# A graph attention and normalisation kernel on one core: late sums and table parts moved, Q's last stores spread over the loads of Q, and four changes of order in the last stage

## What is computed

```python
Q, K, V = ((x @ W).reshape(N, 8, 64) for W in (Wq, Wk, Wv))
score = jnp.einsum('ehd,ehd->eh', K[src], Q[dst]) / 8
score = jnp.exp(jnp.clip(score, -5.0, 5.0))[..., None]
wV = jax.ops.segment_sum(V[src] * score, dst, num_segments=N)
Z = jax.ops.segment_sum(score, dst, num_segments=N)
h = x + (wV / (Z + 1e-06)).reshape(N, D)
mean = jnp.mean(h, axis=0)
var = jnp.mean(jnp.square(h - mean), axis=0)
y = (h - mean) * jax.lax.rsqrt(var + 1e-05) * bn_gamma + bn_beta
out = _layernorm(x + y, axis=-1)
```

## Time and profile before

| what | us |
|---|---|
| median of 3 runs | 1886.88 |
| lowest, highest | 1885.74, 1889.61 |
| the profiled execution | 1886.89 |
| its span, first to last instruction | 1885.0 |
| PE busy | 1843.9 (98%) |
| DVE busy | 1726.0 (92%) |
| ACT busy | 1427.3 (76%) |
| POOL busy | 1235.8 (66%) |
| DMA, mean of the span | 313 GB/s |

### The profile page before, as it was taken

How to read it: one execution, slowest core, us unless ns; L and a number is a source line. 1 busy time by engine, 2 the same in 40 slices (tenths; PEclk the granted TensorE clock), 3 DMA queues, 4 the chain that set the end, 5 groups by cost and what they waited for, 6 DMA issues and landing times.

```text
span 1885.0 us, 41041 instructions
## 1 busy us (share of the span) xinstructions
PE 1843.9 (98%) x7561; PEld 1290.4 (68%) x7672; DVE 1726.0 (92%) x2608; ACT 1427.3 (76%) x4699; POOL 1235.8 (66%) x1424
## 2 busy tenths in 40 slices
PE   8999999998999999999999999999999999999897
PEld 4444444446788887888888888888888888877333
DVE  8877776667999999999999999999999999999898
ACT  1112221126999999999999999999999999998867
POOL 1221112116888888888888888888888888875677
PEclk9999999998999999999999999999999999999999
DMA  5676667658999999999999999999999999999317
GB/s 207 221 252 223 223 222 247 235 195 316 365 364 358 354 356 357 372 357 360 349 365 373 348 354 358 368 357 357 345 368 362 361 360 353 369 360 370 118 34 290
DMA packets 191291, 589.09 MB, mean 313 GB/s; under 512 B 29104, under 2 KB 30864, under 8 KB 191248
## 3 DMA queue, kind: packets, MB, share of 16 engines
q0 software_dynamic: 135904, 465.14, 67.1%
q1 hardware_dynamic: 51888, 121.69, 17.8%
q10 hardware_dynamic: 3456, 1.78, 0.4%
HBM read 535.27 MB, written 78.91 MB: 326 GB/s over the span
## 4 chain that ended last, share of the span: by engine, by line
PE 57%; DVE 23%; issue 7%; DMA 7%; ACT 3%; POOL 2%; ACTq 1%; POOLq 0%; SPq 0%; DVEq 0%
PE places L390 21%; PE acc L1110 21%; PE q_ps L1094 12%; DVE kv L968 9%; DVE raw L979 7%; DMA kv<-kv_d,idx 5%; POOL kv L924 2%; DVE stats L1463 1%; ACT kv L1019 1%; DVE agg L1447 1%; PE mm_ps L1120 1%; DVE agg L1456 1%; DVE raw L972 1%; DMA q_tile<-xb_d 1%; DVE kv L886 1%
## 5 line engine op out<-in xcount | busy, mean ns | idle before, releaser
L924 POOL DMA_INDIRECT kv<-kv_d,idx x880 | 892.8, 1014 | 242.0 <-issue 202.9
L1019 ACT ACTIVATE kv<-kv 128x64 f32<-128x64 f32 x3520 | 889.1, 335 | 14.3
L1110 PE MATMUL acc<-kv,mm_rest 128*128 128x260 f32 x2640 | 634.6, 383 | 3.5 <-POOL kv L886 2.2
L1110 PEld LDWEIGHTS acc<-kv,mm_rest 128*128 128x128 f32 x2640 | 489.9, 189 | 105.1 <-issue 27.7
L968 DVE TENSOR_TENSOR kv<-q_ps,kv 128x1024 f32<-128x1024 f32 x440 | 536.5, 1219 | 16.5 <-DMA kv<-kv_d,idx 10.7
L979 DVE TENSOR_REDUCE raw<-kv 128x16 f32<-128x1024 f32 x440 | 533.1, 1212 | 0.0
L1094 PE MATMUL q_ps<-q_tile,mm_rest 128*128 x1320 | 422.1, 441 | 5.1 <-DVE kv L968 4.9
L390 PE MATMUL places<-w_sb,s_sb 128*128 128x512 f32 x704 | 305.9, 593 | 3.4 <-issue 3.1
L1094 PEld LDWEIGHTS q_ps<-q_tile,mm_rest 128*128 128x128 f32 x1320 | 247.6, 189 | 53.7 <-DVE kv L968 10.4
L886 DVE TENSOR_TENSOR kv<-kv 128x384 f32<-128x384 f32 (+1 forms) x440 | 272.3, 619 | 0.0
L390 PEld LDWEIGHTS places<-w_sb,s_sb 128*128 128x128 f32 x704 | 133.1, 190 | 172.9 <-issue 165.3
(11 more groups left out here) (202 smaller groups left out, 1482.8 us busy)
## 6 DMA issues: line engine op xcount, KB each, us to landing
kv_d<-kv SPq DMA_DIRECT2D x98, 256.0 KB, 2.2
q_tile<-q_d SPq DMA_DIRECT2D x49, 512.0 KB
kv<-kv_d,idx POOLq DMA_INDIRECT x880, 6.4
xb<-in_x POOLq DMA_DIRECT2D x49, 256.0 KB, 4.2
xb_d<-xb POOLq DMA_DIRECT2D x49, 256.0 KB, 6.5
out_rows<-agg SPq DMA_DIRECT2D x49, 256.0 KB, 2.1
x_sb<-in_xT SPq DMA_DIRECT2D x16, 768.0 KB, 6.5
q_d<-q_c SPq DMA_DIRECT2D x16, 512.0 KB, 2.6
```

The costliest lines, as they stand in the source:

```text
L924: pool.indirect_dma_start(kv[:, s, u, 0:2 * DIM], None, kv_d, bass.IndirectOffsetOnAxis(idx[:, s, u:u + 1], 0), bounds_check=N_NODES - 1, ...
L1019: return act.activation(v, v, ACT.Copy, scale=kv[:, s, u, 2 * DIM + h:2 * DIM + h + 1])
L1110: last = pe.matmul(acc[:, bass.ds(par, 1), DIM - (1 - n) * HALF:DIM + n * HALF], m, kv[:, sc, u, DIM + n * HALF:DIM + (n + 1) * HALF], sta ...
```

## The change

Seven edits, which touch no amount of work but four sums.

In `project`: `x_sums_last(0)`, the sum T8 and `ends` are moved behind L753 of trio 0 (`ends` into part 0), and every part of the tables comes two places later, so that trio 0 has only part 0, at its end. SP no longer stores Q of the last trio and of LONE there.

In `attend`: SP loads Q's tiles 2 and 3, then stores the last trio's third tile once tile 3 has landed, and in the same way the three others after tiles 5, 7 and 9. Before the loads from tile 40 on it waits for these stores.

In `normalise`: four pairs more are added on POOL (places 36 with 38, 37 with 39, 40 with 42, 41 with 43) and taken by PE three places later; the last four sums of squares are in another order; the last group's root stands behind the first norm of the group before it; and rows 46 and 48 are normed on DVE, with a semaphore of their own.

```diff
+DVE_NORMS = (TILES - 3, TILES - 1)
@@ project, sync
-                if g == TRIOS - 1:
-                    sp.wait_ge(soft["s_g0"], 32)
-                store_q(c, split_of(g, 2), q_c, s_qc)
...
+                if g < TRIOS - 1:
+                    store_q(c, split_of(g, 2), q_c, s_qc)
...
-            store_q(LONE, TILES, q_d_lone, s_qc)
@@ project, vector
+            def weight_sums_last():
                 dve.tensor_tensor(weight(T8), weight(B11), weight(T13), ALU.add).then_inc(s_wt, 1)
-            def weight_sums_last():
...
-            x_sums_last(0)
-            dve.wait_ge(s_dl, 16)
-            tab(dve.tensor_tensor(ends[:, :], dl[:, :], k128[:, :], ALU.add))
...
-                tables(3 * g)
+                tables(3 * g - 2)
...
                 dve.wait_ge(s_dec, decoded(g, 5))
+                if g == 0:
+                    x_sums_last(0)
...
-                tables(3 * g + 1)
+                tables(3 * g - 1)
...
-                tables(3 * g + 2)
+                tables(3 * g)
@@ attend, sync
+            for n, (t, q, done) in enumerate(last_q):
+                with sp.Fori(2 + 2 * n, 4 + 2 * n) as u:
+                    load_in_turn(u)
+                sp.wait_ge(s_q, 16 * (4 + 2 * n))
+                sp.dma_start(q_d[t * P:(t + 1) * P, :], q[:, :, :].rearrange("p a n -> p (a n)")).then_inc(done, 16)
@@ normalise
+        LATE_PRES = [38, 39, 42, 43]
+            return p + (3 if p in LATE_PRES else AFTER)
...
+            pe.wait_ge(s_sq, TILES - 3)
+            squares(TILES - 4)
+            pe.wait_ge(s_sqp, n + 1)
+            squares(TILES - 6)
+            pe.wait_ge(s_sq, TILES)
+            squares(TILES - 1)
+            pe.wait_ge(s_sqp, n + 2)
+            squares(TILES - 3)
...
+                    if group_of(t) == g and t not in DVE_NORMS:
                         norm(t)
+                        if g == GROUPS - 2 and t == ENDS[g - 1]:
+                            root(g + 1)
...
+                if t >= TILES + 4:
+                    norm(DVE_NORMS[t - TILES - 4])
```

More of the change, by code:

```diff
@@ L54 @@
 SQ_RING = 7
+Q_KEPT = 40
 X_SLOTS = 6
@@ L598, in x_sums_first @@
                 dve.wait_ge(s_x[g % 2], trio_x(g))
+                if g == 1:
+                    dve.wait_ge(s_sums, summed(0, X7))
                 if g:
@@ L648, in tables @@
             def tables(n):
-                if n < VTILES:
+                if n == 0:
+                    dve.wait_ge(s_dl, 16)
+                    tab(dve.tensor_tensor(ends[:, :], dl[:, :], k128[:, :], ALU.add))
+                if 0 <= n < VTILES:
                     visits(n)
@@ L902, in _ @@
                 load(t)
+            sp.wait_ge(soft["s_tb"], 48)
+            for name in ("s_qa", "s_qb", "s_qc"):
+                sp.wait_ge(soft[name], 16 * (TILES // 3 - 1))
+            sp.wait_ge(soft["s_split"], TILES)
+            for n, (t, q, done) in enumerate(last_q):
[3 more added lines that the diff above has]
+                sp.dma_start(q_d[t * P:(t + 1) * P, :], q[:, :, :].rearrange("p a n -> p (a n)")).then_inc(done, 16)
+            with sp.Fori(2 + 2 * len(last_q), Q_KEPT) as t:
+                load_in_turn(t)
+            sp.wait_ge(soft["s_qa"], 16 * (TILES // 3))
+            sp.wait_ge(soft["s_qb"], 16 * (TILES // 3))
+            sp.wait_ge(soft["s_qc"], 16 * (TILES // 3 + 1))
+            with sp.Fori(Q_KEPT, TILES) as t:
+                load_in_turn(t)
             for t in range(FIRST_X):
@@ L1220, in sums_before_pre @@
         def sums_before_pre(k):
-            return sum(not in_pre(n) for n in range(pres[k] + AFTER + 1)) + k + 1
+            return sum(not in_pre(n) for n in range(due(pres[k]) + 1)) + k + 1
         def squares_used(t):
@@ L1263, in _ @@
             for t in range(TILES):
-                sp.wait_ge(s_o, t + 1)
+                if t in DVE_NORMS:
+                    sp.wait_ge(s_od, DVE_NORMS.index(t) + 1)
+                else:
+                    sp.wait_ge(s_o, t + 1 - sum(n < t for n in DVE_NORMS))
                 sp.dma_start(out[t * P:(t + 1) * P, :], row(t)).then_inc(s_out, 16)
@@ L1318, in _ @@
                               stop=p == TILES - 1).then_inc(s_sum, 1)
[L1319 to L1323, removed]
+                for k in range(len(pres)):
+                    if due(pres[k]) == p:
+                        pe.wait_ge(s_pre, k + 1)
+                        pe.matmul(mean_ps, ones[:, :], sq(k % SQ_RING), start=False,
+                                  stop=False).then_inc(s_sum, 1)
             def squares(t):
                 pe.matmul(var_ps, weights(t)[:, :], sq(t % SQ_RING), start=t == 0,
-                          stop=t == TILES - 1).then_inc(s_var, 1)
+                          stop=t == TILES - 3).then_inc(s_var, 1)
             n = 0
-            for t in range(TILES):
-                if t % FIVE == 0 or t == TILES - 1:
+            for t in range(TILES - 6):
+                if t % FIVE == 0:
                     pe.wait_ge(s_sq, t + 1)
@@ L1477, in offset, with norm @@
                                   negate=True).then_inc(s_sh, 1)
+            def norm(t):
+                dve.wait_ge(s_sh, group_of(t) + 1)
+                dve.tensor_scalar(row(t), line(t), mv[:, t, 1:2], shift[:, t:t + 1], ALU.mult, ALU.add).then_inc(s_od, 1)
             for t in range(TILES + 6):
@@ L1526, in program @@
         block = ctx.enter_context(nc.Block())
-        project(nc, block, xT, x, wq, wk, wv, beta, edges, dlast, xb_d, kv_d, q_d, t_d, cnt_d, lb_d, nb_d, tabs, kv, first, soft)
+        last_q = project(nc, block, xT, x, wq, wk, wv, beta, edges, dlast, xb_d, kv_d, q_d, t_d, cnt_d, lb_d, nb_d, tabs, kv, first, soft)
         agg = sb("agg", [P, TILES, AGG], F32)
```

30 lines of the change are left out of this document (14 added, 16 removed).

## The result

| what | us |
| --- | --- |
| before, median of 7 runs | 1886.88 |
| changed, median of 7 runs | 1892.22 (1890.80 to 1895.41) |
| ratio, with its 95% interval | 1.0032 (1.0022 to 1.0041) |
| profiled execution of the changed kernel: time, span | 1895.41, 1893.6 |

The change makes the kernel slower by 0.28% (5.3 us), a little more than the 0.2% that can be told. The time lies in the range on record, 2.8 us above the forecast of 1889.4, and on the slower side of 1890.7, not within 0.2% as the likeliest case had it.

The account below looks back on a forecast made before the run. The prediction took PE and DVE to set the pace together, PE alone in the first stage. Terms -3.05+8.5+1.7-4.8+1.0+0.7-0.3-1.2 = +2.55 on 1886.88 gave 1889.4 us, range 1883.5 to 1894.5.

Parts of the forecast that it names:

- signs of the stall: PE unpaused before 120 us, trio 4 additions waiting 10 us or more, PE idle 7 to 10 near 130, clock 0.5.
- Hole in trio 0: First stage, trio 0: PE's pause at 27.65 closes wholly once work moves behind L753, -3.05 us.
- rival 5: Trio 0: the hole had a slow start that goes with it, 1.65 us more, 1887.7 us; chance 0.02.
- Stall: Trio 4: PE waits for rows that POOL loads late, behind its later wait for `s_visit`, +8.5 us.
- The straight copy: Trio 4: POOL's chain copied at its traced lengths to the later release, PE standing still for 9.6 us.
- rival 3: Row loads land in trio 3's Q stores and next x load, stall 13.5 us, 1894.4 us; chance 0.14.
- Clock behind it: Trio 4: PE's clock falls after the long pause, +1.7 us (0 to 3.3).
- Q's stores: Second stage: moving them ends DVE's first gather waits, -4.8 us; their new place between loads costs +1.0.
- Rival 4: Second stage gives little: PE starts at the lower clock, stores between loads cost 2.8 us, 1892.9 us; chance 0.10.
- Four late pairs: Last stage, mean: no gain from four more POOL sums, a 2.8 us PE pause may drop the clock, +0.7 us.
- Squares: Last stage: the new order of the last squares lets PE go on while POOL sums, -0.3 us.
- End: Last stage: early last root and two rows on DVE relieve ACT by 1.8 us, less store and latency, -1.2 us.

Follow-up runs that it names:

- e1_rows_first: Changed kernel, but POOL does trio 3's row stores and loads before waiting for `s_visit` and making the tables; 2084.55 us, ratio 0.9985 to the kernel before.
- e7_first_stage_only: Kernel before with only the first-stage edits, and trio 3's rows ahead of the tables on POOL; 2082.53 us, ratio 0.9981.
- e5_change_again: Changed kernel run again, unedited, on another chip; 2093.47 us, ratio 1.0034 to the kernel before.
- e3_q_only: Kernel before with only Q's last four stores moved between the loads of Q's tiles; 2088.56 us, ratio 1.0001.
- group 3: Last runs, on one chip: small store on SyncE, trio 3's rows first without late pairs (Q's stores as before, or moved), kernel before; ratios 1.0008, 0.9980, 0.9979, 1.0003.
- the best kernel: Changed kernel with trio 3's rows first on POOL and without the four more pairs of the mean; 2081.37 us, ratio 0.9976 to the kernel before.
- e9_store_on_sp: Changed kernel, wait for the small `t_d` store and two loads moved behind trio 3's rows, that store issued by SyncE; 2068.43 us, ratio 1.0008.
- e12_before: Kernel before itself, unedited, run for its trace on another chip; 2067.10 us, ratio 1.0003.

## Why the prediction came out where it did

**What was right.** The change turns on one hidden link, the part that releases `s_visit`, and this link costs more than the closed hole brings. Forecast for the first stage: +7.15; measured +10.26. The signs of the stall are there: no pause of PE before 120 us, an addition that waits over 10 us for a row (15.55), an idle PE near 130, a clock of 0.50 behind it. Two are off in size: PE is idle for 11.21 us, not 7 to 10, and the fifth pair's multiply comes 2.5 us nearer, not 4.8. `e1_rows_first` shows that this is the cause: one moved call on POOL takes 13.5 us out of the stage.

**Step by step:**

- *Hole in trio 0, -3.05*: measured -3.5 (`e7_first_stage_only`), and -4.2 us in the median there. Right by that pair of traces; the half microsecond more is time in PE's rows about the hole. But rival 5, a slow start behind the hole, got a chance of 0.02 from one trace, and from a row of 28 to 30 us that ends before PE goes on at 30.70. It is in three of the five traces with the hole, at 1.5 to 1.7 us, near the 1.65 named.
- *Stall, +8.5*: measured 11.21 (9.69 in `e5_change_again`). This is the mis-sized term. The straight copy gave 9.6, and I took 1.1 off because the small store would stand behind less. It was not faster (wait 11.91, before 11.17), the rows' stores were waited for 5.15 instead of 3.06, and the last row landed in 4.36, near the 4.6 assumed. The discount had only a guess about traffic behind it. The stall passed the 9.8 that rival 3 named as its point, and the median passed 1890.7 with it: what came true is the slower side of my cases. It was not rival 3's mechanism: the last row load landed in the time assumed, and the extra time lay in the stores ahead of them. And the "quarter of the 3.9 us" would have made 8.6, not 8.5.
- *Clock behind it, +1.7*: 2.61. The loss I had copied came from a stretch with DVE's waits in it; here sixteen products in a row ran after the pause, the first five of them in 4 us.
- *Q's stores, -4.8 + 1.0*: measured -2.5 at the start and +0.5 up to the stage's end in the first pair of traces, and 0 in `e3_q_only` and between the runs of group 3. On the first chip no run had this edit alone. The step that failed is "with them gone both waits should": the waits were DVE's share of a start that is short of gathers, and a later first multiply and a wait for PE took half of their place. Rival 4 had this in its direction. That this is the reason was not tested by itself.
- *Four late pairs, +0.7 (0 to 1.8)*: +1.53. The pause of 2.8 us was 2.67 in every kernel that had the pairs. Whether the clock falls in it decides: in six of the seven kernels with the pairs the six matmuls behind it took 4.54 to 5.49 us, and DVE waited 5.46 to 6.66 us for the mean; in `e1_rows_first` the clock stayed at 1.00, they took 3.60, and DVE waited 4.55. Without the pairs it waited 4.2 to 4.3.
- *Squares, -0.3*: PE's last sum of squares comes 0.4 us nearer to the mean, and -0.26 is left at the end of that stretch. *End, -1.2*: -0.55. ACT's last norm came 1.9 us nearer to its root, as forecast (2.97 us, before 4.89), but SP still had its stores to issue one by one: its last issue came 1.1 nearer, and the last landing took 2.65 us where it took 2.1.

**The sum.** Measured terms of the first execution: -3.5 + 11.2 + 2.6 - 2.0 - 0.4 + 1.5 - 0.3 - 0.6 = +8.5; the medians say +5.3. The two terms that were too small (stall and clock, 3.6 together) and the one that was too favourable (Q's stores, 1.8) all lean to the slower side, and 3 us of them are not in the median. So there is luck in the number: by the terms of the two traces it would have been 1895.4, beyond the range's end of 1894.5. Where the 3 us are was not measured. One candidate is rival 5: if most executions of the kernel before on the first chip had the slow start, which its one trace there has not, the closed hole brought the median 1.6 us more than the traces say.

**Still open.** Where the 3 us between the traces and the medians are, and where the first gather loses its 1.4 us: the first multiply came 10.5 to 13.9 us behind the last K in the kernels with Q's stores moved and 10.5 to 12.8 in those without. Of the clock, why the pause of 2.67 us in the last stage was followed by a fall six times and not once, and that of 3.05 to 3.10 us in trio 0 three times and not twice. Whether the gain of the best kernel is as large on a chip like the first wasn't measured.

## What to carry to other kernels

When a step moves later in one engine's list, look for the semaphore that it releases, and read what the waiting engine has queued behind that wait; here 3.5 KB of table held up three rows of x and through them the matrix engine. Copy such a chain at its measured length and take nothing off for traffic that you imagine away. Whether the clock falls behind a short pause differed here from one execution to the next, so one trace does not settle it: look into every trace that has the pause. A wait that a profile puts on a transfer is worth its length only if the engine behind it is not short of the same transfers a moment later.

## What the runs showed of the hardware

- While a store of 3.5 KB in single words was under way, the DMA engines of all queues stood at a share of 0.77 and moved 23 GB/s, for 5 us; stores of 256 KB issued beside it, on the same queue or another, were waited for up to 10 us instead of 3 to 5. The Trainium skill's page "DMA: Bandwidth & Descriptors", section "Rules for kernel authors", says that such a store becomes one descriptor for each element. No run here changed its form, so that this is the cause is not shown; that neighbours on another queue pay too is what `e9_store_on_sp` adds.
- A pause of 3.05 to 3.10 us in trio 0, behind 14 us of products without a gap, was followed by a fall of the granted clock in three of five traces (0.50 from 31 to 33 us in `e12_before`, where the first trace has 1.00) and by none in two. One of 2.67 us in the last stage was followed by a fall in six of seven kernels, and those of 4.28 and 5.37 us in trio 4 were too. The five have the same products before and behind the pause, so what PE had done ahead of it does not tell them apart.
- The same kernel took 1887 us on one chip and 2066 to 2088 on three others. Its first and last stages were equal to within 3 us; only the stage of gathers differed, 1313 against 1496 to 1516 us, at 358 against 315 GB/s.
